# One of twelve readout products moved from VectorE to GpSimd, a ring of eight scan buffers, and the x1 sum split from the output projection

## The reference

```
xs  = four orders of silu(conv(x @ in_proj))           # 192 channels, 196 tokens, 4 directions
dts, Bs, Cs = split(xs . x_proj)                       # 16 states: B and C per state and token
dts = softplus(dts . dt_projs + bias)
h   = h * exp(dts * A[n]) + (dts * xs) * B[n]          # for each state n, a scan over tokens
y   = sum over n of h * C[n]  (+ D * xs)               # "readout": product with C, sum over states
y   = norm(sum of directions) * g + b, times silu(z), then y @ out_proj
out = x + y
```

## Time and profile before

| | us |
|---|---|
| median of 3 runs | 3129.97 |
| the profiled execution | 3124.29 |
| its span, first to last instruction | 3122.5 |
| DVE busy | 2624.9 (84%) |
| PE busy | 2718.1 (87%) |
| POOL busy | 2142.9 (69%) |
| ACT busy | 1812.7 (58%) |
| DVE scans (1536) | 1405.4 |
| DVE readouts (768) | 745.6 |

### The profile page before, as it was taken

How to read it: one execution, slowest core, us unless ns; L and a number is a source line. 1 busy time by engine, 2 the same in 40 slices (tenths; PEclk the granted TensorE clock), 3 DMA queues, 4 the chain that set the end, 5 groups by cost and what they waited for, 6 DMA issues and landing times.

```text
span 3122.5 us, 100405 instructions
## 1 busy us (share of the span) xinstructions
PE 2718.1 (87%) x39088; PEld 2026.1 (65%) x39088; DVE 2624.9 (84%) x4163; ACT 1812.7 (58%) x3812; POOL 2142.9 (69%) x1816
## 2 busy tenths in 40 slices
PE   4999999999996788888888888888888888888886
PEld 3999999996654465665655656556566656656554
DVE  6444444445999999999999999999999999999995
ACT  1111111112226777777777777777777777777774
POOL 5333333331006888988889888988989889888883
PEclk9999999999998999999999999999999999999999
DMA  5000000002335455454554555555555555545541
GB/s 207 0 0 0 0 0 0 0 0 82 139 133 176 139 164 179 142 177 145 168 165 149 165 159 164 161 168 156 158 168 151 163 165 150 180 144 172 173 125 48
DMA packets 57087, 385.30 MB, mean 123 GB/s; under 512 B 10100, under 2 KB 15060, under 8 KB 31700
## 3 DMA queue, kind: packets, MB, share of 16 engines
q1 hardware_dynamic: 57044, 384.79, 39.8%
HBM read 352.64 MB, written 32.11 MB: 123 GB/s over the span
## 4 chain that ended last, share of the span: by engine, by line
POOL 35%; issue 28%; PE 26%; DVE 8%; ACT 1%; POOLq 1%; DMA 0%; DVEq 0%; ACTq 0%
POOL arena L495 22%; PE ps L1138 10%; PE ps L1147 10%; PE ps L1179 3%; POOL arena L468 3%; POOL arena L477 3%; POOL arena L482 3%; POOL arena L472 3%; DVE arena L789 2%; DVE arena L786 2%; PE ps L1134 2%; DVE conv_out L202 1%; POOL arena L460 1%; DVE stats L571 1%; POOL arena L455 1%
## 5 line engine op out<-in xcount | busy, mean ns | idle before, releaser
L1268 PE MATMUL ps<-arena,ident 128*128 128x392 f32 (+1 forms) x4096 | 1164.3, 417 | 0.9 <-DVE arena L798 0.9
L980 ACT ACTIVATE ps<-arena,abias,a 128x390 f32<-128x390 f32 x1024 | 688.7, 677 | 306.0 <-DVE arena L789 177.0
L1268 PEld LDWEIGHTS ps<-arena,ident 128*128 128x128 f32 x4096 | 683.3, 191 | 144.3 <-issue 1.3
L798 DVE TENSOR_TENSOR arena<-arena,ps 128x784 f32<-128x784 f32 x768 | 745.6, 971 | 28.0 <-PE ps L1258 1.8
L786 DVE TENSOR_TENSOR_SCAN arena<-ps,arena 128x392 f32<-128x392 f32 x768 | 702.7, 956 | 7.5 <-issue 4.4
L789 DVE TENSOR_TENSOR_SCAN arena<-ps,arena 128x392 f32<-128x392 f32 x768 | 702.7, 957 | 0.0
L1258 PE MATMUL ps<-arena,sel 96*128 96x196 bf16 x3072 | 391.7, 250 | 307.9 <-DVE arena L798 307.4
L1258 PEld LDWEIGHTS ps<-arena,sel 96*128 96x128 bf16 x3072 | 230.4, 98 | 612.4 <-DVE arena L798 578.0
L495 POOL TENSOR_TENSOR arena<-arena 128x784 f32<-128x784 f32 x256 | 474.2, 1852 | 133.2 <-PE ps L1268 130.8
L984 ACT ACTIVATE ps<-arena,abias,a 128x195 f32<-128x195 f32 x1024 | 474.6, 504 | 136.3 <-DVE arena L786 69.3
L495 POOL TENSOR_TENSOR arena<-arena,wh_sb 128x784 f32<-128x784 f32 x256 | 472.7, 1852 | 71.8 <-PE ps L1268 69.7
(11 more groups left out here) (180 smaller groups left out, 3025.9 us busy)
## 6 DMA issues: line engine op xcount, KB each, us to landing
wx_sb<-b_by_state SPq DMA_DIRECT2D x64, 1568.0 KB, 6.3
wh_sb<-b_by_state SPq DMA_DIRECT2D x64, 1568.0 KB, 6.3
arena<-b_by_image SPq DMA_DIRECT2D x128, 784.0 KB, 9.0
arena<-x_seq SPq DMA_DIRECT2D x4, 2352.0 KB, 16.1
x_in<-x_pair SPq DMA_DIRECT2D x16, 588.0 KB, 4.2
x_dram<-x SPq DMA_DIRECT2D x16, 588.0 KB, 3.1
x<-x_dram SPq DMA_DIRECT2D x16, 588.0 KB, 10.0
out<-xhat SPq DMA_DIRECT2D x16, 588.0 KB, 2.9
```

Of the source, the lines that this page charges most:

```text
L798: dve.tensor_tensor(h, h, bank(3), ALU.mult).then_inc(s["readout_ready"], 1)
L980: ins = act.activation(r, src, ACT.Exp, scale=a01[:, c:c + 1], bias=abias01[:, c:c + 1])
L1268: mm = pe.matmul(ps[:, 5 if g < 8 else 6, 0:cols], ident[:, :], h[:, m * cols:(m + 1) * cols], start=(opens and m == 0), stop=(closes and ...
```

## The change

- `RING` becomes 8; the two added buffers lie outside the arena.
- Group 7 (`POOL_READS`) has no readout on DVE. POOL multiplies its buffer by C (`pool_read`) after it has done drive 10 of the same stage, once both scans of group 7 are done. C comes by DMA: SP writes the four rows of C from `xdbl` to `c_by_state` in DRAM beside the B values and reads them back, spread over all partitions, to `c_chunk` (128 x 784) with `spread_c`, after the second B chunk of the next stage. SP waits there until POOL has read the old values.
- PE leaves out the spread for group 7, spreads C for group 8 one iteration earlier, and sums group 7 after group 9 (iteration 10). The semaphore counts and the place in `reduced` that a drive waits for follow this order.
- `residual` goes one group later than `out_proj`, and the first `out_proj` goes from (2, 6) to (2, 5).

```diff
-RING = 6
+RING = 8
+POOL_READS = (7,)
+READ_LEAD = 3
+BEHIND = 2
@@ block.sync
+                for q, g in enumerate(POOL_READS):
+                    for img in range(2):
+                        sp.dma_start(c_by_state[k][q, :, img, :], xdbl[N * img + 2 * g:N * img + 2 * g + 2, T:T2]
+                                     ).then_inc(s["c_spilled"], 16)
+            def spread_c(P, k, first=False):
+
+                sp.wait_ge(s["c_spilled"], (P + 1) * (32 * len(POOL_READS)))
+                if not first:
+                    sp.wait_ge(s["pool_read"], P * len(POOL_READS))
+                rows = c_by_state[k].rearrange("q n i t -> (q n i t)").unsqueeze(0)
+                sp.dma_start(c_chunk[:, :], rows.broadcast_to([128, len(POOL_READS) * GC])).then_inc(s["c_chunk_in"], 16)
@@ block.gpsimd
                 if not early:
-                    pool.wait_ge(s["reduced"], G - (RING - 1))
+                    before = st * GRP + g - RING
+                    place = before // GRP * GRP + ORDER.index(before % GRP)
+                    pool.wait_ge(s["reduced"], G - (st * GRP + g) + (place + 1))
+            def pool_read(P, st, g, G):
+
+                _, _, view = group_aps(g)
+                h = view(hb[(st * GRP + g) % RING])
+                q = POOL_READS.index(g)
+                if q == 0:
+                    pool.wait_ge(s["c_chunk_in"], P * 16 + 16)
+                pool.wait_ge(s["scan_done"], G * 2 + 2)
+                pool.tensor_tensor(h, h, view(c_chunk[:, q * GC:(q + 1) * GC]), ALU.mult).then_inc(s["pool_read"], 1)
@@ POOL's loop over the groups
                         drive(P, st, g, i * (K4 * GRP) + (st * GRP + g), head and st * GRP + g < RING)
+                        if g - READ_LEAD in POOL_READS:
+                            pool_read(P, st, g - READ_LEAD, i * (K4 * GRP) + (st * GRP + (g - READ_LEAD)))
                         if (st, g) == (2, 4) and not head:
                             normed(i - 1)
@@ DVE's loop
-                        read_out(st, g, G)
+                        if g not in POOL_READS:
+                            read_out(st, g, G)
@@ PE's loop
-                        spread(g, st)
-                        if not opening:
+                        if g in POOL_READS:
+                            spread(g + 1, st)
+                        elif g - 1 not in POOL_READS:
+                            spread(g, st)
+                        if not opening and (g - 1) % GRP not in POOL_READS:
...
+                        if g - 1 - BEHIND in POOL_READS:
+                            r = g - 1 - BEHIND
+                            pe.wait_ge(s["pool_read"], P * len(POOL_READS) + (POOL_READS.index(r) + 1))
+                            reduce(st, r)
...
-                            if (st, g) in ((2, 6), (3, 4), (3, 6)):
+                            if (st, g) in ((2, 5), (3, 4), (3, 6)):
                                 out_proj(i - 1, (g // 2 - 1) if st == 3 else 0)
+                            if (st, g) in ((2, 6), (3, 5), (3, 7)):
                                 residual(i - 1, (g // 2 - 1) if st == 3 else 0)
```

More of the change, by code:

```diff
@@ L55, in build @@
     b_by_image = nc.dram_tensor("b_by_image", [K4, 2, N, T], F32)
+    c_by_state = nc.dram_tensor("c_by_state", [K4, len(POOL_READS), 2, 2, T], F32)
     with ExitStack() as ctx:
@@ L76, in build @@
         ident = sb("ident", [128, 128])
+        c_chunk = sb("c_chunk", [128, len(POOL_READS) * GC])
         sel = sb("sel", [96, N, 3, 128], BF16)
@@ L140, in build @@
         wh_cols = wh_sb[:, :, :, :].rearrange("p a b c -> p (a b c)")
-        hb = [carve(GC) for _ in range(RING)]
+        hb = [carve(GC) for _ in range(RING - 2)] + [sb(f"hb_{q}", [128, GC])[:, :] for q in range(2)]
         b_chunk = [wx_cols[:, 0:CHUNK], wh_cols[:, 0:CHUNK], carve(CHUNK)]
@@ L186, in build @@
             "oproj_ready", "o_ready", "out_stored", "fin_z", "fin_x1",
-            "b_spilled", "b_chunk0", "b_chunk1", "b_chunk2", "skipped")}
+            "b_spilled", "b_chunk0", "b_chunk1", "b_chunk2", "skipped",
+            "c_spilled", "c_chunk_in", "pool_read")}
         def conv_taps(eng, i, taps, q):
@@ L216, in group_aps, with reduce_order @@
                     lambda a: a.rearrange("p (m q t) -> p m q t", m=2, q=2))
+        def reduce_order():
+            order, late = [], []
+            for g in range(GRP):
+                if g in POOL_READS:
+                    late.append(g)
+                else:
+                    order.append(g)
+                order += [r for r in late if r + BEHIND == g]
+            return order
+        ORDER = reduce_order()
         def half_cols(hf):
@@ L321, in _ @@
                 spread_b(0, 0, j, True)
+            spread_c(0, 0, True)
             spill_z(PAIRS - 1)
@@ L352, in pair @@
                         next_x(i)
+                    if ahead and max(POOL_READS) + READ_LEAD < 8:
+                        spread_c(P1, k1)
                     if ahead:
                         spread_b(P1, k1, 1)
+                    if ahead and max(POOL_READS) + READ_LEAD >= 8:
+                        spread_c(P1, k1)
                     if st == 3 and not head:
@@ L797, in read_out @@
                 dve.wait_ge(s["c_ready"], G + 1)
-                dve.tensor_tensor(h, h, bank(3), ALU.mult).then_inc(s["readout_ready"], 1)
+                dve.tensor_tensor(h, h, bank(3), ALU.mult).then_inc(s["readout_ready"], 1 + (g + 1 in POOL_READS))
             def pair(i, head, last):
@@ L935, in read_bc @@
                     act.wait_ge(s["b_spilled"], P * 48)
+                    act.wait_ge(s["c_spilled"], P * (32 * len(POOL_READS)))
                 act.activation(xdbl[:, :], ps[:, 7, 0:T2], ACT.Copy).then_inc(s["xdbl_ready"], 1)
@@ L1258, in spread @@
                     mm = pe.matmul(ps[:, 3 + m // 2, m % 2 * T:m % 2 * T + T], sel[:, n, kind, :], rhs, start=True, stop=True)
-                mm.then_inc(s["c_ready"], 1)
+                mm.then_inc(s["c_ready"], 1 + (g + 1 in POOL_READS))
             def reduce(st, g):
@@ L1265, in reduce @@
                 cols = GC // runs
-                opens, closes = st % 2 == 0 and g in (0, 8), st % 2 == 1 and g in (7, 11)
+                tile = [r for r in ORDER if (r < 8) == (g < 8)]
+                opens, closes = st % 2 == 0 and g == tile[0], st % 2 == 1 and g == tile[-1]
                 for m in range(runs):
@@ L1350, in pair @@
                         if not head:
-                            if (st, g) in ((0, 4), (1, 5), (2, 6), (3, 4)) and ahead:
+                            if (st, g) in ((0, 4), (1, 5), (2, 5), (3, 4)) and ahead:
                                 pe.wait_ge(s["dt_read"], P1 * 4 + 4)
```

## The result

The changed kernel takes 3160.63 us (median of 4 runs, 3155.24 to 3162.96) against 3130.48 us: 1.0093 times as long (95% interval 1.0076 to 1.0111). The profiled execution takes 3155.24 us, its span is 3152.3 us, 29.8 us more than before.

A forecast was written before the change was run, and what follows sets the result against it. DVE bounds the kernel before; after the change, a closed POOL-DVE loop through POOL's in-order queue. 3124.3 + 32.1 (stage 2) - 2.5 (rounds) - 0.9 (last stage) = 3153.0, plus 5.7 to the median: 3159 us, range 3143 to 3180.

The forecast's parts named there:

- The saving that goes into a wait: Each stage: DVE saves group 7's readout, 0.89 us, then waits 0.85 us for POOL at the next stage's group 0.
- The round: Closed loop POOL, DVE, POOL, once a stage: 21.13 + 11.86 = 32.99 us against 33.03, a gain of 0.04 us.
- the release of DVE by POOL: End of POOL's drive 0 to DVE's start of the next stage: taken as 0.04 us.
- a margin of 0.3 us: Stage 0, PE iteration 10: the spread for group 11 is 0.3 us ahead of its readout; cost taken as nothing.
- Stage 2: Late `normed` delays ACT's `affine` and group 3's decays: DVE stalls 2.14 us in pairs 1 to 15, 32.1 us.
- The sum: Whole kernel: 3124.3 + 32.1 - 2.5 - 0.9 = 3153.0 us profiled, median 5.7 us above, so 3159 us.
- The sum by spans: Chain by the profile's spans instead of start-to-start spacings: 11.45 us, round 32.58 us, 28 us less in the sum.
- the ring: Ring of eight costs and gives nothing, since the product's wait cuts POOL's lead at three groups.
- the split: `residual` one group later takes 0.66 us from one group to the next; worth nothing by itself.
- the load of C: SP's new load, a quarter of a B chunk's bytes, has some 30 us of time: costs nothing.
- Rival (a): DVE keeps its saving, POOL's chain being hidden: 3130 - 57 = 3073 us; chance 0.07.
- rival (c): Product and drives beside it take 2.00 us, chain 0.57 us longer: 3207 us; chance 0.07, shared with other added waits.

The follow-up runs named there:

- experiment 2: Changed kernel with READ_LEAD 4 instead of 3, so POOL's product stands after drive 11 instead of drive 10: 3084.34 us.
- experiment 4: Changed kernel without POOL's product (group 7 summed without being multiplied by C), its waits made waits for group 7's scans, load of C kept: 3080.22 us.
- experiment 6: Changed kernel, ring of six, with the product made twice in the same place, once into an unread scratch buffer: 3270.23 us.
- experiment 8: Changed kernel with READ_LEAD 4 and, in stage 0, ACT's second centring read at g = 9 (was 8) and PE's skip sum at 11 (was 10): 3070.00 us.
- Experiment 1: Changed kernel with `affine` one group later in ACT's queue in stage 2, behind the decays of group 3: 3137.56 us.
- Experiment 3: Changed kernel with RING 6 instead of 8: 3157.78 us.
- experiment 5: Kernel before, with a ring of eight and `residual` one group behind `out_proj`, no product on POOL: 3128.66 us against 3128.53.
- experiment 7: Changed kernel with READ_LEAD 4 (product after drive 11) and RING 6: 3086.90 us.

## Why the prediction was right

- **The saving that goes into a wait.** It said that DVE saves 0.89 us and waits 0.85 us at the next stage; the waits are 0.90 to 0.94 us, at three of four stages. The saving itself was a little larger, 0.97 us (33.03 to 32.06 us in experiments 2 and 4): the 0.89 us are the readout alone, and two scans that follow each other directly are 0.86 us apart, a scan and its readout 0.98 us. In a closed loop this only makes the wait longer. It had put POOL's queue, not its load, in the place of the bound, and experiments 2, 4 and 6 show that: the same load, placed one drive later, is worth 76 us.
- **The round.** Predicted 32.99 us, measured 33.09 to 33.20 us. The term that was too small is the release of DVE by POOL: 0.04 us was taken, for which no row was given, but DVE starts 1.98 us after drive 0 does (2104.32 and 2106.30 in the changed kernel's timelines), 1.85 + 0.13. So the gain of 0.04 us a round is a loss of 0.07 us. In stage 0 it is 0.1 us more, since there DVE itself is the bound: the readout of group 11 is held up by 0.38 us, by the spread behind two sums and the skip. The prediction gave this spread a margin of 0.3 us and took the cover as good; it wasn't. It also missed that ACT's second centring step, which waits for PE, makes the decays of group 9 0.67 us late once DVE comes 0.89 us earlier. In the changed kernel these two stand in place of the wait for POOL at the start of stage 1, and so cost next to nothing; in experiment 2 they come to light (stage 0 lasts 33.19 us, the others 32.06), and experiment 8 gets 14 us back.
- **Stage 2.** Predicted a stall of 2.14 us and a round of 35.13 us, measured 1.92 us and 35.08 us. Experiment 1 confirms the cause, and also the number that was worked out beside it: POOL would reach the product 1.1 us before the scans are over; it waits 1.21 us there, and this is what `affine` one group later gains (1.20 us per stage 2).
- **The sum.** The difference of the spans, 29.8 us, is made of 32.9 us in the 14 pairs of the loop (134.46 instead of 132.11 us each); -1.7 us since the first stage starts earlier (965.78 instead of 967.49); -0.5 us in the first pair, whose rounds outside the hardware loop are shorter (32.8 us); -3.1 us in the last pair; and +2.2 us in the tail after it. The prediction had 28.7 us from 32.1 - 2.5 - 0.9: its pairs in the loop were 0.36 us too short (134.10 us), 5 us in 14, and the start, the ends and the tail, which it didn't work out, gave 4 us back. That the totals agree to 2 us is partly luck; the two mechanisms are not.
- **The last pair**, which follows the hardware loop in a copy of its own, is where most of this luck lies. It has the stall of stage 2 too, and so should have been longer. But in the kernel before its stage 0 lasted 41.16 us, with two waits that no other stage has, and in the changed kernel 36.98 us, with one of 3.98 us (also with nothing in the profile that ended it, "issue"). The rows are of the kernel before:

```profile
2961.82 1.84 DVE L786 TENSOR_TENSOR_SCAN arena<-ps,arena 128x392 f32<-128x392 f32 x2 [3.05 <-ACT ps L980]
2982.82 1.84 DVE L786 TENSOR_TENSOR_SCAN arena<-ps,arena 128x392 f32<-128x392 f32 x2 [4.39 <-issue]
```

  In each profile but that of experiment 6 this stage is 3 to 8 us longer than its like in the loop. What holds the engines up there was not tested. The tail, too, has two lengths whatever the kernel: from the last scan on it is 33.6 to 34.2 us before and in experiments 1, 3, 4, 5 and 7, and 35.9 to 36.2 us in the changed kernel and in experiments 2, 6 and 8. In the changed kernel its mean granted clock is 0.85, in the kernel before 0.90 of full speed. Experiment 3 has the change and the short tail, so the 2.2 us don't belong to the change.
- **The sum by spans.** The prediction says that its total by the profile's spans would be 28 us less; from its own rounds, 32.99 and 32.58 us, it is 63 x 0.41 = 26 us. The product and all behind it took 9.85 us from start to start (2061.25 to 2071.10) against 9.87 us in the prediction, which bears out the spacings.
- **What it took as nothing** held: the ring (experiments 3, 5), the split (5) and the load of C (4, where it is still there). What it took as nothing and was not are the two holdups of stage 0. Rival (a), the full saving of 57 us, is about what the kernel gives with the product placed after drive 11 and these two moved (58.5 us; 45 us without moving them, 3129.3 - 3084.3).

## What to carry to other kernels

Before work is moved to an engine with time to spare, write down its queue from the moved step to the next thing that the bounding engine waits for: an in-order queue that must wait for the bounding engine's newest result starts everything behind it late, whatever its load. Put such a step as far back in the queue as its reader allows, and measure lead (how long before its use a thing is ready), not busy share; a lead that is lost shows up at third engines too, as ACT's `affine` here. A saving on the bound also takes the cover from small holdups elsewhere (here two in stage 0, worth 14 us in all), which are then worth a run of their own.

## What the runs showed of the hardware

The product on GpSimd has the same spacing as the drives, 1.80 us for 128 x 784 in place, with VectorE's scans beside it, and a second one in the same place makes a stage 1.74 us longer. The release of VectorE by GpSimd takes 0.13 us by the profile's ends, more than the 0.03 us of ScalarE's release by GpSimd before (3104.81 + 1.43 to 3106.27), near the 0.04 us that the prediction took; what makes the difference stays open. TensorE's mean granted clock in the profiled executions was 0.993 before and in experiments 1 and 4, 0.987 in the changed kernel and 0.970 with the product twice. In the pairs of the changed kernel's loop it cost nothing that shows: 13 of 14 last 134.45 to 134.49 us, and one 134.20. With the product twice it cost some 6 us (experiment 6).

There is one stretch in which the two engines do slow each other. Ahead of the scan part VectorE's convolution steps (L202) run beside the drives of the earlier trace rows, both with two operands from SBUF. In the kernel before, beside the drives and after them:

```profile
953.95 8.17 DVE L202 SCALAR_TENSOR_TENSOR conv_out<-pad,par,conv_out 128x196 f32<-128x196 f32 x4
964.50 3.06 DVE L202 SCALAR_TENSOR_TENSOR conv_out<-pad,par,conv_out 128x196 f32<-128x196 f32 x7
```

Beside the drives it is four steps in 8.17 us, one for each drive, and once the drives are over seven steps in 3.06 us. So VectorE's steps get over four times slower and GpSimd's drives only a tenth (2.00 instead of 1.81 us). That the operands are the reason was not tested apart. Of this nothing is seen between GpSimd's product and VectorE's scans, which read one operand from PSUM, so rival (c) of the prediction, which had it there, is out.
